# State-space stage: C weighting of unit 13 moved from GpSimd to VectorE

## The reference, cut to what matters

```
def step(h, inp):
    d_t, B_t, C_t, u_t = inp
    dA = jnp.exp(d_t[:, :, None] * A)
    h = h * dA + (d_t * u_t)[:, :, None] * B_t[:, None, :]
    y = jnp.einsum('bdn,bn->bd', h, C_t)
    return (h, y)
...
_, ys = jax.lax.scan(step, h0, xs)
y = jnp.swapaxes(ys, 0, 1) + x_conv * D
y = y * _silu(z)
return jnp.einsum('bld,md->blm', y, out_proj_w)
```

## Time and profile before

| | before |
|---|---|
| median of 3 runs | 6730.61 us (6730.06 to 6731.73) |
| the profiled execution: its own time, its span | 6723.96 us, 6722.2 us |
| busy over the whole span: PE, DVE, ACT, POOL | 6022.6, 4123.5, 3519.3, 5282.3 us |
| state-space scans, first to last start | 71.4 to 3609.9 us |

### The profile page before, as it was taken

The page is one execution under the profiler, slowest core; times in us unless marked ns, Lnnn a source line. Parts: engine busy times, 40 slices in busy tenths (PEclk is TensorE's granted clock), DMA queues, the critical chain, the costliest instruction groups (busy, mean ns, idle before and its releaser), DMA issues. The chain is left out here.

```text
span 6722.2 us, 77307 instructions
## 1 busy us (share of the span) xinstructions
PE 6022.6 (90%) x24804; PEld 3844.6 (57%) x24804; DVE 4123.5 (61%) x4999; ACT 3519.3 (52%) x6417; POOL 5282.3 (79%) x4084
## 2 busy tenths in 40 slices
PE   7999999999999999999996999900599999999999
PEld 3444444444444444444444888800488888888888
DVE  6999999999999999999995677730000000000000
ACT  6676767676767676767764788700122222222222
POOL 6999999999999999999997877547555455555554
PEclk9999999999999999999998999955799999999999
DMA  3555555555555454555543344400355666556554
GB/s 125 167 165 166 165 170 164 167 168 169 167 165 170 162 170 164 166 166 170 166 161 105 99 125 123 137 12 1 124 185 181 182 187 187 184 182 180 181 169 132
DMA packets 556867, 1029.83 MB, mean 153 GB/s; under 512 B 82546, under 2 KB 250996, under 8 KB 521904
## 3 DMA queue, kind: packets, MB, share of 16 engines
q1 hardware_dynamic: 441168, 669.34, 30.8%
q0 software_dynamic: 115296, 355.56, 17.5%
HBM read 926.04 MB, written 88.88 MB: 151 GB/s over the span
## 5 line engine op out<-in xcount | busy, mean ns | idle before, releaser
L361 POOL TENSOR_TENSOR m_dbu<-m_du,m_bb 128x1024 f32<-128x1024 f32 x1024 | 2398.0, 2380 | 0.0
L739 PE MATMUL m_y_bank<-m_prod,m_ident 128*128 128x512 f32 x4096 | 1977.0, 612 | 143.5 <-POOL m_prod L370 143.5
L512 ACT ACTIVATE m_decay<-m_delta,m_a_neg 128x512 f32<-128x512 f32 x2048 | 1419.6, 695 | 724.5 <-DVE m_h L622 722.5
L739 PEld LDWEIGHTS m_y_bank<-m_prod,m_ident 128*128 128x128 f32 x4096 | 788.9, 196 | 1123.0 <-issue 906.8
L622 DVE TENSOR_TENSOR_SCAN m_h<-m_decay,m_h_end,m_dbu 128x512 f32<-128x512 f32 x1024 | 1258.9, 1266 | 3.5 <-ACT m_decay L512 2.5
L1682 DVE TENSOR_SCALAR e_ye<-e_ybank,e_listing 128x256 f32<-128x256 f32 x270 | 118.2, 479 | 1817.9 <-PE e_ybank L1716 1817.9
L622 DVE TENSOR_TENSOR_SCAN m_h<-m_decay,m_dbu 128x512 f32<-128x512 f32 x1024 | 1196.6, 1205 | 14.0 <-ACT m_decay L512 13.4
L1668 ACT ACTIVATE e_a<-e_ubank 128x512 f32<-128x512 f32 x540 | 322.5, 597 | 1473.2 <-PE e_ubank L1707 1473.2
L370 POOL TENSOR_TENSOR m_prod<-m_h,m_cb 128x1024 f32<-128x1024 f32 x416 | 989.3, 2378 | 19.2 <-issue 14.6
L1707 PE MATMUL e_ubank<-e_xT,e_w 128*128 128x256 f32 x4320 | 978.2, 380 | 1.3 <-ACT e_xT L1659 1.3
L1716 PE MATMUL e_ybank<-e_w,e_a 128*128 128x256 f32 x4320 | 954.5, 379 | 0.7 <-ACT e_a L1668 0.7
(11 more groups left out here) (198 smaller groups left out, 6430.7 us busy)
## 6 DMA issues: line engine op xcount, KB each, us to landing
m_bb<-rows_bc SPq DMA_DIRECT2D x1024, 256.0 KB, 3.7
m_cv<-rows_bc SPq DMA_DIRECT2D x608, 256.0 KB, 3.9
m_cb<-rows_bc SPq DMA_DIRECT2D x416, 256.0 KB, 3.4
m_xin<-in_x SPq DMA_DIRECT2D x32, 512.0 KB, 5.7
m_xres<-in_x SPq DMA_DIRECT2D x32, 512.0 KB, 5.3
x<-m_xres SPq DMA_DIRECT2D x32, 512.0 KB, 5.9
a_xa<-x SPq DMA_DIRECT2D x64, 256.0 KB, 2.8
a_xr<-x SPq DMA_DIRECT2D x64, 256.0 KB, 3.1
```

Of the source, the lines that this page charges most:

```text
L361: nc.gpsimd.tensor_tensor(dbu[:, slot], du[:, q[1], p * PC:(p + 1) * PC], bb[:, slot].unsqueeze(1).to_broadcast([P, PC, T]), ALU.mult).the ...
L512: nc.scalar.activation(decay[:, cc], delta[:, r, c], ACT.Exp, scale=a_neg[:, c, n:n + 1]).then_inc(decay_done, 1)
L739: ins = nc.tensor.matmul(y_bank[:, cc], ident[:], prod[:, slot, cc], start=False, stop=(n == NS - 1))
```

## The change

Unit 13 leaves `POOL_UNITS` and so enters `VECTOR_UNITS`. There are 12 POOL units and 20 DVE units in a block in place of 13 and 19.

```
-    POOL_UNITS = [u for u in range(UNITS) if u % 5 in (1, 3)]
+    POOL_UNITS = [u for u in range(UNITS) if u % 5 in (1, 3) and u != 13]
```

## The result

The changed kernel takes 6777.28 us (median of 6 runs, 6772.77 to 6778.11), the kernel before 6730.34 us beside it (6 runs, 6728.12 to 6731.73). The ratio is 1.0068, 95% interval 1.0055 to 1.0081: slower by 46.9 us. The forecast was 30.6 us more, 6761. The time lies in the range of 6722 to 6780, 3 us from its upper end, and just over the forecast's own 6750 to 6776. The profiled execution took 6778.11 us, its span 6776.2.

The account below looks back on a forecast made before the run. A chain through POOL, PE, ACT and DVE was taken to bound the kernel, 0.5 us a block longer than POOL's own work. 16 x 0.79 + 16 x 1.12 = 30.6 us gave 6761.2 us, range 6722 to 6780.

Parts of the forecast that it names:

- Worth: 0: POOL's saved weighing, 2.32 us a block, only becomes a longer wait ahead of weighing 21, so it gains nothing.
- DVE's term: DVE's added weighing behind scan (14,0) costs 0.79 us in a half-0 block and 1.12 us in a half-1 block.
- PE. ... Cost 0: PE gets unit 13's product no later; its 1.44 us wait at the start of pass 1 grows by 0.79, costing nothing.
- the chain: Round of a block: POOL weighing 21 to 31, PE, ACT's copy of C, DVE to scan (21,1), POOL again; 110.94 us on average.
- part 2 of the chain: PE waits 2.96 us for weighing 31's product, then works without a gap, including the projection that ACT takes.
- a wait for ACT: Upper end of the forecast's own range: a wait for ACT of 0.3 us a block adds 10 us, giving 6776.
- ACT's copy: ACT gains one copy of C a block, 0.58 us, with 1.4 us of cover at the first; cost 0.
- SP's queue: Load of B of unit 5, queued behind a C row, taken as hidden; rival: 1 us late, 32 us more, 6793 us, chance 0.08.
- a sign of being wrong: Listed for the next profile: POOL waiting for B of unit 5, among other signs.
- POOL's waits: Wait ahead of weighing 21 grows from 0.78 and 0.21 us to about 3.9 and 3.6 less earlier waits, some 110 us.
- POOL paces: Rival: POOL sets the pace, its round drops 2.32 us until DVE bounds; 6665 us, or 6708 us; faster by over 0.2%: 0.12.
- The delay is swallowed: Rival: DVE's 1.12 us vanish in its wait at the gate of pass 1; no change, 6731 us, chance 0.13.

Follow-up runs that it names:

- the matmuls in both kernels: Two unread matmuls a block ahead of PE's wait for unit 31, added to the kernel before (6717.49 us) and to the changed kernel (6744.29 us).
- the third buffer: Changed kernel with POOL's last C row in a third buffer of its own again: 6770.76 us, ratio 1.0065 to the kernel before.
- the kernel without the product: Kernel before with unit 13 weighed by nobody, POOL's weighing removed and none added on DVE: 6728.16 us, ratio 0.9996.
- unit 8: Kernel before with unit 8 moved from POOL to DVE in place of unit 13: 6731.84 us, ratio 1.0006.
- units 26, 28, 21: Move to DVE at unit 26 or 28 in place of 13, against the kernel before: 6731.23, 6728.47 us; at unit 21, with two further edits: 6713.58 us.
- the version with unit 21: Kernel before with two unread matmuls, ACT's copy of C of unit 10 made earlier, and unit 21 moved to DVE: 6713.58 us, ratio 0.9979.

## Why the prediction was right, and where its size was off

**Direction and its reason: right, and shown.** "Worth: 0" for POOL's relief is 0.9996 when done alone. DVE's added weighing is 1.0069 when done alone, the ratio of the whole change, and in every block of the changed kernel weighing 21 starts 0.13 us behind scan (21,1).

**DVE's term: right.** 0.79 and 1.12 us a block were forecast, 0.73 and 1.14 are in the table, (0.73 + 1.14) / 2 x 32 = 29.9 us. With the matmuls in both kernels the difference is 26.8 us.

**"PE. ... Cost 0", with its wait at the start of pass 1 that "grows by 0.79, and it is off the chain": this is the step that fell short.** The wait grew by 0.68 us (1.44 to 2.12), and it is off the chain itself. But what PE did behind it was not the same work at the same speed. The low clock behind this wait delays PE to unit 28; that takes away the wait and the low clock there, and PE then idles 2.96 us ahead of unit 31, on the chain. The forecast took part 2 of the chain over as it was, 32.68 us, and it became 34.26, about 1.4 to 1.8 us more in 13 of the 15 half-0 to half-1 rounds. By the means of 29 rounds, the part 10 to 21 grew by 0.94 us, which is DVE's, and the part 31 to 10 by 0.61, the clock's. The mean round grew by 1.58, and 29 x 1.58 = 45.8 of the 46.9 us measured: some 27 are DVE's and some 18 the clock's, a term that the sum had at nothing. The trace of before could have warned twice. Its half-1 blocks had a gate wait of 1.93 us, a low clock behind it, and the slow part behind weighing 31; the forecast's own 1.44 + 0.79 = 2.23 us put the half-0 blocks above that wait. And the two matmuls of unit 31 take 3.47 us behind a wait of 2.96 us in one half and 1.99 us behind 1.27 us in the other, so this part of the chain had two lengths, 34.10 and 32.68 us, and I had looked at it as one.

**The range held partly by luck.** Its upper part, from 6766 to 6776, was made for a wait for ACT, which is not there; what filled it was the clock.

**ACT's copy and SP's queue: cost 0, right.** In none of the 30 blocks is there a wait ahead of the weighings of 13 to 15. POOL did wait for a B row, which was named as a sign of being wrong, but 4 times and 2.4 us in all, and with the third buffer, which took these waits away, the loss stayed.

**POOL's waits.** "3.9 and 3.6 us less what it waits earlier", some 110 us in all: 1.70 us ahead of weighing 16 and 1.84 or 1.21 ahead of 21, and 123.9 us in all; the round that the clock made longer adds to them. "Weighing 21 comes each 111.9 us": 111.91 in one kind of block, 113.38 in the other, for the reason above.

**The rivals.** "POOL paces" fell: its condition, that POOL did not wait for DVE at 21, is false by the 0.13 us and by the kernel without the product. The rule of the Trainium skill, "Perfetto Trace Analysis", section "Identifying the Most-Contended Engine", which sends the reader to the engine with the highest occupancy, would have given 6656 us; the run gave 6777, and the relief alone 6728. The trace agrees that POOL is the fullest, with 99.5%, and the relief alone speaks against the conclusion. "The delay is swallowed" fell too. It does happen at unit 8, where a wait follows. "SP's queue" fell, by the kernel with the third buffer.

**My expectations of units 26, 28, 21 missed by more than the prediction did.** I took a gain on the engine that is the chain as a gain of the round, and did not look for the next chain close under it.

**Open.** Why some blocks kept the full clock behind a wait of 2.96 us, whether the third buffer has a part in how many do, and what sets the pace of the version with unit 21.

## What to carry to other kernels

When three engines are 95% busy or more, look for the wait that each has once in a round, and price a moved instruction by where it stands to those waits: the same weighing cost nothing ahead of a wait, and behind it 0.73 or 1.14 us a round on DVE and 1.58 on average with the clock. When a change shifts an engine's idle time, follow what runs behind that time and at which granted clock, although the wait itself is off the chain. And an edit that gains on the chain is worth no more than the distance to the next one: 0.5 us of 110.9 between the chain and POOL's own work here. Relieving POOL between 21 and 31 gained nothing.

## What the runs showed of the hardware

- TensorE's granted clock fell behind waits of 1.93 us (to 0.60 over 4.3 us), 2.12 us (0.62 over 4.0 us), 2.50 us (0.71 over 5.8 us) and 2.96 us (0.54 over 3.4 us), and not behind those of 0.80, 1.25 and 1.27 us. Behind 1.44 us it stayed at 1.00 in the kernel before. But the length of a wait alone doesn't decide. In the changed kernel's early blocks a wait of 2.96 us was followed by matmuls at full speed:

```profile
976.78 1.98 PE L739 MATMUL m_y_bank<-m_prod,m_ident 128*128 128x512 f32 x4 [2.96 <-POOL m_prod L370]
```

And in the kernel before with two added matmuls, PE's wait of 1.44 us for the gate was followed by 0.62 in one block and by 1.00 in another:

```profile
1022.20:1026.20 4.00, 3.91 (x6) 1.80 (x7) 4.00 (x5) 2.67 (x6) 4.00 (x2) 0.62 0.68 222
799.70:803.70 4.00, 3.96 (x9) 1.82 (x10) 4.00 (x4) 2.67 (x6) 4.00 (x2) 1.00 0.66 211
```

- Two or three matmuls of no use, put into such a wait, gave time back: two gave 11 us of 6728 in the kernel before and 33 of 6777 in the changed one. Three, which in a third of the blocks made the sum of unit 31 some 1.1 us late, gave 20 us in place of 33.
